# From attention to experts: the last two strips projected from where they are made, and the order of SP's list at the change of stage

## What is computed

```python
xn = layernorm(x)                       # x: 8 rows (batch) of 512 tokens, 256 wide
kqv = xn @ W_kqv + b_kqv                # 16 heads of 16
attn = softmax(q @ k.T / 4 + alibi bias, causal)
y = (attn @ v) @ W_proj + b_proj
probs = softmax(xn @ Wg)                # 8 experts
# each expert takes its 512 best tokens; a token chosen by several goes to the
# likeliest of them, one chosen by none to its own best expert
out = gate * (gelu(xn @ W1[e]) @ W2[e]) # e, gate: the token's expert and its chance
return x + y + out
```

## Time and profile before

| | us |
|---|---|
| median of 3 runs | 636.27 (627.75 to 658.72) |
| profiled execution | 632.95 |
| its span | 631.2 |

### The profile page before, as it was taken

One profiled execution on the slowest core, in us unless ns is written; L12 is line 12 of the kernel. 1 busy time (PEld: TensorE's weight loads), 2 busy tenths in 40 slices (PEclk: granted clock), 3 DMA queues, 4 the chain that ended last, 5 costly groups with the idle time before them and its releaser, 6 DMA issues.

```text
span 631.2 us, 11893 instructions
## 1 busy us (share of the span) xinstructions
PE 509.6 (81%) x4071; PEld 300.1 (48%) x4071; DVE 459.2 (73%) x876; ACT 346.3 (55%) x655; POOL 339.5 (54%) x479
## 2 busy tenths in 40 slices
PE   1889896658888989989868957898877678999991
PEld 1445553324343544535424523544313467999980
DVE  4897647959999899898898999997333225666661
ACT  2546552217656666757645645575765324666660
POOL 8696220404634455455453554487884217777773
PEclk9999999969988998989988989998979787999996
DMA  5477788494323353463432342476659545766520
GB/s 175 147 200 169 239 277 271 154 299 116 118 78 90 111 165 86 127 169 93 146 102 67 110 131 69 137 237 197 191 170 367 90 107 116 139 145 140 135 77 17
DMA packets 102793, 94.27 MB, mean 149 GB/s; under 512 B 38657, under 2 KB 89921, under 8 KB 102725
## 3 DMA queue, kind: packets, MB, share of 16 engines
q1 hardware_dynamic: 92462, 71.92, 40.8%
q0 software_dynamic: 6576, 17.91, 9.4%
q10 hardware_dynamic: 3696, 3.67, 1.8%
HBM read 44.35 MB, written 40.05 MB: 134 GB/s over the span
## 4 chain that ended last, share of the span: by engine, by line
PE 36%; DVE 20%; POOL 12%; SPq 10%; issue 8%; DMA 7%; ACT 5%; POOLq 0%; DVEq 0%; ACTq 0%
DVE mx L894 7%; PE ps L1346 7%; PE ps L1202 5%; PE ps L1336 4%; PE ps L1119 4%; PE ps L1191 4%; PE ps L1217 3%; PE ps L1172 3%; POOL pr_all L627 3%; POOL w_low L595 2%; PE ps L1337 2%; SPq L412 2%; SPq L319 2%; POOL sorted_rows L608 2%; PE ps L1169 2%
## 5 line engine op out<-in xcount | busy, mean ns | idle before, releaser
L763 ACT ACTIVATE pr_all<-ps 128x512 f32<-128x512 f32 x320 | 182.3, 599 | 143.5 <-PE ps L1191 142.3
L894 DVE TENSOR_REDUCE mx<-ps 128x2 f32<-128x768 f32 (+1 forms) x192 | 155.5, 859 | 18.7 <-PE ps L1172 17.6
L627 POOL TENSOR_SCALAR_AFFINE_SELECT pr_all<-pr_all 128x384 f32<-128x384 f32 x128 | 64.9, 531 | 133.9 <-ACT pr_all L763 133.7
L1191 PE MATMUL ps<-qs,ks 128*128 128x512 f16 (+2 forms) x448 | 118.0, 336 | 14.4 <-DMA qs<-cc 5.7
L1169 PE MATMUL ps<-maxmask,idb 128*128 128x256 bf16 (+1 forms) x320 | 84.6, 264 | 44.6 <-DVE mx L894 33.1
L1172 PE MATMUL ps<-ks,qs 128*128 128x384 f16 (+3 forms) x512 | 117.8, 316 | 0.0
L1202 PE MATMUL ps<-pr_all,vt 128*17 128x512 f32 (+3 forms) x1024 | 85.7, 454 | 6.5 <-POOL pr_all L630 6.4
L1191 PEld LDWEIGHTS ps<-qs,ks 128*128 128x128 f16 x448 | 38.9, 100 | 87.1 <-ACT pr_all L763 55.8
L1169 PEld LDWEIGHTS ps<-maxmask,idb 128*128 128x128 bf16 x320 | 32.1, 101 | 74.6 <-DVE mx L894 43.0
L1346 PE MATMUL ps<-vt,pr_all 128*128 x312 | 59.7, 279 | 6.2 <-DVE pr_all L1081 6.2
L1336 PE MATMUL ps<-pr_all,xnp 128*128 128x256 f16 x312 | 57.8, 279 | 4.5 <-DMA pr_all<-sorted_rows 4.5
(11 more groups left out here) (180 smaller groups left out, 916.4 us busy)
## 6 DMA issues: line engine op xcount, KB each, us to landing
qs<-q_parts SPq DMA_DIRECT2D x64, 100.0 KB
ks<-k_parts SPq DMA_DIRECT2D x64, 96.0 KB
sorted_rows<-ecmp POOLq DMA_DIRECT2D x1, 5160.0 KB, 22.8
k_parts<-pr_all SPq DMA_DIRECT2D x16, 256.0 KB, 2.7
q_parts<-pr_all SPq DMA_DIRECT2D x16, 256.0 KB, 2.8
xr<-in_L_attn_x_dram SPq DMA_DIRECT2D x8, 512.0 KB
w_h<-in_L_ffn_W_dram SPq DMA_DIRECT2D x16, 256.0 KB, 3.1
w_l<-in_L_ffn_W_dram SPq DMA_DIRECT2D x16, 256.0 KB, 2.9
```

Source lines behind the costliest of these rows:

```text
L627: pool.affine_select(out=v, in_=v, compare_op=ALU.is_ge, fill=0.0, base=0, pattern=[[0, 3], [1, P]], channel_multiplier=-1).then_inc(sel_m ...
L763: act.activation(dst, src, ACT.Exp, scale=SCORE).then_inc(exp_made, 1)
L894: last = dve.tensor_reduce(mx[:, n1 % 2, :, 2 * g + c, t], ps[:, 2 * (u % 2):2 * (u % 2) + 2, c0:c0 + w], AX, ALU.max)
L1191: last = pe.matmul(out, ks[:, p, c, t * P:(t + 1) * P], rhs, start=True, stop=True, skip_group_check=True)
```

## The change

- `x` of the last row no longer goes through `xr`. It gets its own buffer `x_last`, which takes the space of four tables that the router has read for the last time by then. SP loads it at (6, 1) and POOL adds the bias at (7, 2).
- Strips 30 and 31 are not packed. PE reads them in `yn` with its blocks of 32 partitions and multiplies with `wp_wide`: the projection's weights for these strips, spread to the same partitions, with zeros in between. `wp_wide` takes the space of `rec_wide`; POOL zeroes it at G = 22 and SP loads the weights at (6, 1) with four DMAs.
- `pack(28)` goes at (7, 2), `pack(29)` at (7, 3).
- SP behind the loop: four row loads with `store_sum(6)` after the second, four token loads, then it waits for the last row's sum and stores it in two halves; then the remaining row and token loads.
- PE behind the loop: the first half of the last row's projection, the codes and `find_up(0)`, `with_v(31)`, strip 30, `up(0)`, strip 31, `up(1)`, `up(2)`, `down(0)`.
- DVE sums the last row ahead of `sum_up(0)`.

```diff
--- before.py
+++ after.py
@@ -28,6 +28,7 @@
 HID = 3
 
 ROWS_FIRST = 3
+ROWS_EARLY = 4
 TILES = NT + X
 
 WORK = TILES - 1
@@ -132,10 +133,10 @@
         maxmask = sb("maxmask", [P, P], BF16)
         bits = sb("bits", [P, BITS // 2, 3], U32)
         epst = sb("epst", [P, 1], F32)
-        seg = sb("seg", [P, X, NT], F32)
-        rank8 = sb("rank8", [P, X, NT], F32)
-        lim = sb("lim", [P, X, NT], F32)
-        sno = sb("sno", [P, TILES, X], F32)
+        tables = sb("tables", [P, 3 * X * NT + TILES * X], F32)
+        seg, rank8, lim = (tables[:, i * X * NT:(i + 1) * X * NT].rearrange("p (e t) -> p e t", e=X) for i in range(3))
+        sno = tables[:, 3 * X * NT:].rearrange("p (s e) -> p s e", e=X)
+        x_last = tables[:, 0:TB * E].rearrange("p (t e) -> p t e", t=TB)
         iot = sb("iot", [P, TILES * X], I32)
         w_h = sb("w_h", [P, EC, 3 * E + X], F16)
         w_l = sb("w_l", [P, EC, 3 * E + X], F16)
@@ -189,6 +190,7 @@
 
 
         posi = rec_wide[:, :].bitcast(I32)
+        wp_wide = rec_wide[:, :].rearrange("p (g n) -> p g n", g=2)
         c_rows = ysb[:, 0, :].bitcast(F16)[:, 0:S]
         K_POS, K_ONES = slice(0, 3), slice(32, 34)
         K_FAR, Q_FAR = slice(64, 64 + 2 * FARS), slice(96, 96 + 2 * FARS)
@@ -273,6 +275,7 @@
         apart = sem("apart")
         zrows_in, bias_made, xb_made = sem("zrows_in"), sem("bias_made"), sem("xb_made")
         yp_in, xr_made = sems("yp_in", NG), sem("xr_made")
+        x_last_in, wide_zero, wide_in = sem("x_last_in"), sem("wide_zero"), sem("wide_in")
         zeros, marks_read, tot_read = sem("zeros"), sem("marks_read"), sem("tot_read")
         prt_made, thr_made = sem("prt_made"), sem("thr_made")
 
@@ -445,9 +448,18 @@
                         sp.dma_start(w2_l, ws_d[:, :, 1, 1, :].rearrange("x p w -> p x w")).then_inc(w2_in, 16)
                     if g == 3 and n < B - 1:
                         shift_rows(n + 1)
-                    if g == 3:
+                    if (n, g) == (B - 2, 1):
+                        sp.wait_ge(pos_made, 2)
+                        sp.dma_start(x_last, x_t[B - 1]).then_inc(x_last_in, 16)
+                        sp.wait_ge(wide_zero, 1)
+                        for j in range(HG):
+                            sp.dma_start(wp_wide[32 * j:32 * j + D], w_proj.rearrange("(g j d) n -> j d g n", g=NG, j=HG)[j, :, 2:4, :]
+                                         ).then_inc(wide_in, 16)
+                    if (n, g) in ((B - 1, 2), (B - 1, 3)):
+                        pack(NG * n + g - 2)
+                    elif g == 3:
                         pack(NG * n)
-                    if g == 3 and n > 0:
+                    if g == 3 and 0 < n < B - 1:
                         store_sum(n - 1)
                         sp.wait_ge(xa_out, 16 * n)
                         load_x(n)
@@ -465,15 +477,19 @@
 
             sp.wait_ge(y_made, NG * B - 1)
 
-            strips = {1: NG * B - 3, 2: NG * B - 2, 3: NG * B - 1}
-            for q in range(SLOTS):
+            for q in range(ROWS_EARLY):
                 load_rows(q, q)
-                if q in strips:
-                    pack(strips[q])
-                if q % 2:
-                    load_tokens(q - 1, q - 1)
+                if q == 1:
+                    store_sum(B - 2)
+            for q in range(AHEAD):
+                load_tokens(q, q)
+            for j in range(2):
+                sp.wait_ge(xadd_made, TB * (B - 1) + 2 * j + 2)
+                sp.dma_start(xa_t[B - 1][:, 2 * j:2 * j + 2], x_last[:, 2 * j:2 * j + 2]).then_inc(xa_out, 16)
+            for q in range(ROWS_EARLY, SLOTS):
+                load_rows(q, q)
+                if q >= AHEAD:
                     load_tokens(q, q)
-            store_sum(B - 1)
             for s in range(SLOTS, SLOTS + ROWS_FIRST):
                 sp.wait_ge(h_made, s - SLOTS + 1)
                 load_rows(s, s % SLOTS)
@@ -601,8 +617,12 @@
                 pool.tensor_tensor(yn[:, G % 2, :], ysb[:, G % 2, :], rec_wide[:, :], ALU.mult).then_inc(y_normal, 1)
 
             def add_bias(n):
-                pool.wait_ge(xr_in, 16 * (n + 1))
-                pool.tensor_tensor(xr[:, :, :], xr[:, :, :], xb[:, None, :].broadcast_to([P, TB, E]), ALU.add).then_inc(xr_made, 1)
+                if n < B - 1:
+                    pool.wait_ge(xr_in, 16 * (n + 1))
+                else:
+                    pool.wait_ge(x_last_in, 16)
+                rows = xr[:, :, :] if n < B - 1 else x_last
+                pool.tensor_tensor(rows, rows, xb[:, None, :].broadcast_to([P, TB, E]), ALU.add).then_inc(xr_made, 1)
 
             def scatter(t):
                 pool.indirect_dma_start(out=xs_words, out_offset=bass.IndirectOffsetOnAxis(ap=pos[:, t:t + 1].bitcast(U32), axis=0),
@@ -633,6 +653,10 @@
                             expert_low(NQ * (n + 1) + g)
                     if 2 <= G < TURNED + 2:
                         normalise(G - 2)
+                    if G == TURNED + 2:
+                        pool.memset(wp_wide, 0.0).then_inc(wide_zero, 1)
+                    if (n, g) == (B - 1, 2):
+                        add_bias(B - 1)
                     if n == 0 and g == 1:
                         pool.wait_ge(xb_made, 1)
                         add_bias(0)
@@ -644,7 +668,6 @@
                     if (n, g) in SCATTERS:
                         for t in range(PER_EXPERT):
                             scatter(PER_EXPERT * SCATTERS.index((n, g)) + t)
-            add_bias(B - 1)
 
             def tile_c(s, k, q):
                 wait_apart(pool, xs_in[q], 16 * (k + 1))
@@ -661,7 +684,7 @@
 
             pool.wait_ge(y_made, NG * B)
             mark(pool.memset(xg[:, :, :], 0.0))
-            pool.wait_ge(xa_out, 16 * B)
+            pool.wait_ge(xa_out, 16 * (B + 1))
             for q in range(AHEAD):
                 tile_c(q, 0, q)
             for k in range(0, WORK // SLOTS):
@@ -1090,14 +1113,14 @@
 
             invert(NG * B - 2)
             invert(NG * B - 1)
+            dve.wait_ge(xr_made, B)
+            for j in range(2):
+                dve.wait_ge(pj_made, TB * (B - 1) + 2 * j + 2)
+                v = x_last[:, 2 * j:2 * j + 2, :]
+                dve.tensor_tensor(v, bank[7 - 2 * j].rearrange("p (t e) -> p t e", t=2), v, ALU.add).then_inc(xadd_made, 2)
             sum_up(0)
             sum_up(1)
             low(0)
-            dve.wait_ge(xr_made, B)
-            for j in range(2):
-                dve.wait_ge(pj_made, TB * (B - 1) + 2 * j + 2)
-                v = xr[:, 2 * j:2 * j + 2, :]
-                dve.tensor_tensor(v, bank[7 - 2 * j].rearrange("p (t e) -> p t e", t=2), v, ALU.add).then_inc(xadd_made, 2)
             sum_up(2)
             low(1)
             for s in range(WORK):
@@ -1349,28 +1372,38 @@
                 last.then_inc(o_made, 1)
 
 
-            with_v(NG * B - 1, range(TB))
+            def last_dst(t):
+                return bank[7 - 2 * (t // 2)][:, t % 2 * E:(t % 2 + 1) * E]
+
+            def last_strip(G):
+
+                pe.wait_ge(y_normal, G + 1)
+                for t in range(TB):
+                    last = pe.matmul(last_dst(t), yn[:, G % 2, t * P:(t + 1) * P], wp_wide[:, G % 2, :], start=False,
+                                     stop=(G == NG * B - 1), skip_group_check=True)
+                    if G == NG * B - 1:
+                        last.then_inc(pj_made, 1)
+
+            pe.wait_ge(exp_made, NSJ * NG * B)
+            pe.wait_ge(xadd_made, TB * (B - 1))
+            for t in range(TB):
+                project(B - 1, t, (0,), last_dst(t), begin=(t % 2 == 0))
             pe.wait_ge(pos_made, 2)
-            pe.wait_ge(exp_made, NSJ * NG * B)
-            pe.wait_ge(w1_in, 16 * X)
             code = [experts_of(k) for k in range(-(-WORK // SLOTS))]
             e = [expert(code[s // SLOTS], s % SLOTS) for s in range(WORK)]
             find_up(0)
+            with_v(NG * B - 1, range(TB))
+            pe.wait_ge(wide_in, 16 * HG)
+            last_strip(NG * B - 2)
+            pe.wait_ge(w1_in, 16 * X)
             up(0, e[0])
+            last_strip(NG * B - 1)
             find_up(1)
-            pe.wait_ge(xadd_made, TB * (B - 1))
-
-            def last_row(i):
-                for t in range(TB):
-                    project(B - 1, t, (i,), bank[7 - 2 * (t // 2)][:, t % 2 * E:(t % 2 + 1) * E], begin=(t % 2 == 0))
-
-            last_row(0)
             up(1, e[1])
             find_up(2)
             pe.wait_ge(y_copied, NG * B)
             up(2, e[2])
             find_down(0)
-            last_row(1)
             pe.wait_ge(w2_in, 32)
             for s in range(WORK):
                 if s + HID < WORK:
```

## The result

The changed kernel took 624.27 us (median; 623.48 to 624.57), the kernel before 634.31 over its runs so far (627.75 to 658.72). The plain medians are 10.0 us apart, but the kernel before also has a slower state, to which its 658.72 belongs, and by the fast runs alone the ratio is 0.9888, with a 95% interval of 0.9843 to 0.9934: 1.1% or 7 us less, between 4 and 10. The two profiled executions differ by 8.6 us in their spans (631.2 and 622.6), the forecast was 11.6.

The account below looks back on a forecast made before the run. POOL, full from its first gather, was taken to set the end; that gather 11.8 us earlier, less 0.2 for the memset, gave 11.6 us off 632.95, or 621.3. From the runs' median 624.7; named 622.5, range 613 to 631.

Parts of the forecast that it names:

- step 1: SP's packing and loads around the loop's end: PE has strips 28 and 29 at 488.6, bounds 483.9 and 499.
- step 3: Expert codes and `find_up(0)` moved ahead of `with_v(31)` on PE: 4.2 us from 488.8, so it starts at 493.0.
- POOL full from its first gather on: POOL's gathers and scatters fill it from the first gather, forecast at 506.4, for 103.75 us, ending at 610.2.
- Step 2: PE projects strips 28 and 29 before `with_v(31)`: eight records of 0.22 us, 1.7 us.
- Step 4: `with_v(31)` on PE: 2.35 us at the high clock, 4.7 at the low, taken as 4.1, ending at 497.1.
- Steps 5 and 6: PE's last two strips end at 501.8, DVE's sum at 502.6, SP's store lands at 505.5, first gather 506.4.
- What is late next: After the sum: `down(0)` at 505.7, PE done at 605.0, POOL at 610.2 still decides; rows 4 to 7 covered.
- Off the path: SP's loads at (6,1) and `add_bias(7)` at (7,2) cost nothing; POOL's memset at most 0.45 us, charged 0.2.
- cheap registers and a high clock: Rival, chance 0.22: register work costs 0, `with_v(31)` 2.4 us; first gather 502.2, time 617, from 614 to 620.
- Low clock all through: Rival, chance 0.15: `with_v` 4.7 us, strips 3.4 each, `up(0)` 2.6; first gather 511.7, time 626.7 to 630.
- a late strip 29: Slower rival, chance 0.05: PE queues behind strips 28 and 29; at 499 they eat 10.4 of 11.6 us; 637.

## Why the prediction was right, point by point

The time, 624.27, lies 1.8 us above the 622.5 named and well within 613 to 631; a change within 2% was held the likeliest. The fall of 7 us by the ratio (8.6 by the spans) was forecast as 11.6, so the nearness of the time is in part luck: the sum gave 621.3, and 622.5 was chosen above it. The mechanism was right, an early gather with POOL full behind it; the gather came 2.9 us later than forecast. A start of `with_v(31)` after 495 was named beforehand as the sign that step 1 or step 3 was wrong, and it started at 495.22.

- **POOL full from its first gather on, and 103.75 us from there to the end:** right on this chip, 103.93. It was read from one execution on one chip and it holds there. On the other three chips it does not, with 139 to 146 us. That the result was measured on a chip of the first kind is luck as well.
- **Step 1, strips 28 and 29 at 488.6:** the mis-sized term. Strip 29 was in at 490.5, 2.0 us later. The place in the queue was right, the landing was not the same: 7.4 us behind the start of its last issue, where 5.3 were taken over from strip 28 before. The second w2 load landed 0.8 us later too (470.50 + 16.7 = 487.2 against 470.71 + 15.7 = 486.4). From the second w2 load's issue to strip 29 it was 20.0 us on this chip, and 19.2 to 19.8 in four traces of other chips, while the time from its own last issue went from 7.4 to between 4.4 and 5.0. Before, strip 28 took 17.9 from there. That fits the wait behind w2 that the prediction assumed, and 2 us of what stands in between were missing. New in between are strip 28's own four DMAs, and the transposing row loads now go out at 483.68, before strip 29 is in, where they went out at 489.91 before. Which of these it is has not been tested.
- **Step 2 and 3, the projection and the registers, `with_v(31)` at 493.0:** it started at 495.22, 2.0 of it from step 1. From the arrival of strip 29 to `with_v(31)` 4.4 us were given, and it was 4.6. That this came out is in part luck. The prediction gave the projection 1.7 us, at the high clock, and the low clock only to `with_v(31)` behind it; in fact the projection took 3.75, so of the register work only 0.86 us stuck out. By the row, taking it away on this chip would bring less than 1 us. Where the projection was short, 4.8 to 5.4 us lay between its start and `with_v(31)`, and without the register work the gap is gone. No row separates the loads from the operations. By the figure of the Trainium skill (DMA: Bandwidth & Descriptors, Latency and other measured facts) the five loads would be an estimated 3.0 us, which no run here shows apart from the rest.
- **Step 4, the clock:** 4.47 us instead of 4.1, and 0.6 us more on strip 30 (2.26 against 1.7). Right in kind, 0.9 us too small. With PE kept busy both are at 2.35 and 2.0.
- **Steps 5 and 6:** strip 31's y was ready at 502.58, before `up(0)` ended; the last strip ended 3.2 us late for the reasons above. From the sum's end, 505.79, to the first gather it is 3.55 us, where 3.8 were given.
- **What is late next:** `down(0)` at 508.91, 3.1 us behind the sum, as worked out (505.7 for 502.6); PE ended at 608.7, 4.6 us before POOL. The rows of tiles 4 to 7 were never waited for.
- **Off the path:** strips 28 and 29 cost SP more than was counted. The four issues of strip 28 took 8.33 us instead of 2.5, one of them 6.4. It cost nothing, as SP would have waited for the scatters until 480.5. `add_bias` fitted: it ran from 479.16, and the selects behind it started at 481.75 instead of 481.83, in a loop that runs 0.3 us earlier there; the scores still ended 0.3 us earlier. DVE's product beside it began first, at 479.13, and took its usual 0.42, while `add_bias` took 2.63 instead of 2.34. By the Trainium skill (SBUF — State Buffer, Who interferes with whom), the order of issue decides which of the two engines is blocked. The trace agrees (0.42 undisturbed for the first, 0.29 us more for the second), and the order fell the cheap way.
- **The rivals:** cheap registers and a high clock are out, as `with_v(31)` started at 495.22 and took 4.47 us. Low clock all through held for the projection and `with_v(31)`, and not for strips 30 and 31, with 2.26 and 1.95 us where 3.4 each were given. The one that would have made it slower, a late strip 29, is real as a mechanism and had 2 of the 11.6 us it needed.

## What to carry to other kernels

Where a wait is taken off one chain, look at what now stands in front of that chain's first link on the same engine: here the projection of two strips and the register loads were put ahead of the matmul that everything waits for, and the register work alone kept 4.9 us of the gain on one chip. Register loads belong where the engine waits anyway. Read which engine is full from its first instruction to its last: where POOL was, the first gather moved by 8.8 us and the span fell by 8.6. But take that reading on more than one chip before it carries a forecast, since on three others POOL wasn't full and small gains in the distance didn't show in the time.

## What the runs showed of the hardware

- One DMA issue of 32 KB on SP held its queue for 6.4 us, right behind two loads of 2 MB; the same issue takes 0.6 otherwise. The four of that strip took 8.33 us, and 5.2 to 6.7 in the traces of the other chips, where four take 2.4 to 2.5 elsewhere.
- The changed kernel took 1.07 times as long on another chip (666.74 us and 624.27), the kernel before on three others (676 to 680 and 634). PE's records of `up` (L1359) hardly differed, 0.286 us on average and 0.273 (525 to 600 us); most of the time went into idle stretches of up to 5 us in the experts' stage, whose cause no row gives.
- 24 matmuls whose result nobody reads, run in PE's wait in 5.34 us, kept the granted clock at 1.00, which is 2.4 GHz: `with_v(31)` behind them took 2.35 us instead of 3.9 to 4.5.
